# RWKV block times a routed expert layer: the experts' second product in three f32r passes instead of one f32 product

## The chip, the cores and the metric

The kernel runs on one core of a Trainium2 chip. The time is the device time of one launch in microseconds. The kernel before took 1147.42 us, the median of three runs (1146.86 to 1148.62).

## What is computed

The input is x, 16 sequences of 512 tokens with 256 channels; both branches read its layer norm xn. They are an RWKV block over the tokens of a sequence in order (time mixing with a decaying state, then channel mixing) and a layer of 8 experts in which every token goes to one expert. Cut to what matters here:

```python
x = L0_attn_x                      # (16, 512, 256): T = 8192 tokens
xn = _layernorm(x, axis=-1)
s = _L0_attn_ref(xn, ...)          # layer norms, k/v/r projections, wkv scan, Wo, channel mix
# _L0_ffn_ref(xn, Wg, W1, W2): D = 256, F = 512, E = 8
probs = jax.nn.softmax(xt @ Wg, axis=-1)
# the T // E best tokens of each expert, the rest by their largest probability: tok2exp, weights
for e in range(E):
    gate = jnp.where(tok2exp == e, weights, 0.0)
    h = jax.nn.gelu(xt @ W1[e], approximate=False) @ W2[e]
    out = out + gate[:, None] * h
g = _silu(out)
x = x + s * g
```

The change touches `... @ W2[e]`, a product over F = 512.

## The kernel before

The program has two stages. The first, some 820 us, goes through 16 blocks of 512 tokens: norms, projections, scan and channel mixing, with the router's work spread between them; its last block ends with `channel_out(NB - 1, ...)` on TensorE. It writes x and s as rows to DRAM (`xs_rows`) and a list of tokens sorted by expert, padded so that each tile of 128 tokens belongs to one expert.

The second stage, the expert stage, goes through NT = 72 such tiles. Each engine runs its own `step(t, i, g)`: six steps written out, a loop (`Fori`) of ten rounds of six, and six written out again. Engines meet only at semaphores, and each takes its instructions in the order in which they stand:

- GpSimd fetches the rows of a tile by an indirect DMA (`gather`, six tiles ahead) and stores finished rows (`scatter`).
- ScalarE in step t: `xn(t+3)` (line 690) normalises the rows with two numbers of `info_t`; `gelu(t+1)` (line 697) takes 128x512 from PSUM; `tanh(t)` (line 705) takes the second product.
- TensorE in step t: `turn_x(t+2)` (line 936) transposes; `mlp_in(t+1)` (line 946) is the first product, 8 matmuls 128x128; `mlp_out(t)` (line 957) the second, 4 matmuls 128x256 in f32.
- VectorE in step t: `mlp_input(t+3)` copies the expert's W1 (line 1507, its place read from `expert_at` into a register, line 1504) and the transposed tile out of PSUM (line 1509); `combine(t)` (lines 1519 to 1525) waits for `tanh(t)` and makes the output rows; `take_index(t+6)` (line 1436) and `take_info(t+4)` (line 1441) copy from the list.

So `xn(t+4)`, the first instruction of ScalarE's step t+1, waits (`info_ready`) for `take_info(t+4)`, the last of VectorE's step t, which stands behind `combine(t)`.

One product in the first stage is already done in three f32r passes: `hidden` splits the mixed input into a high part, rounded to f32r by ScalarE (line 589), and the rest, made by VectorE (line 1301), and multiplies high by high, high by low and low by high (lines 845 to 852). The matmul instructions of f32 stand twice in the trace for each one in the code (4 matmuls of `mlp_out` are x8), those of f32r once.

## Time and profile before

| | |
|---|---|
| median of three runs | 1147.42 us |
| the profiled execution's own time | 1145.82 us |
| its span, first to last instruction | 1144.0 us |
| TensorE busy (share of the span) | 1056.0 us (92%) |
| VectorE busy | 878.3 us (77%) |
| ScalarE busy | 627.6 us (55%) |
| GpSimd busy | 353.9 us (31%) |
| mean granted TensorE clock | 0.98 of full |

The engines' shares are means over both stages; the stage to read is the expert stage, from 850 us on. Rows of the timeline give the start, the duration and, in brackets, how long the engine had been idle and what ended that. A duration begins and ends inside the engine's pipeline, so that the next instruction of the engine can start some 0.1 us before the end shown.

### The profile page before, as it was taken

The numbers are of one execution on the slowest core, as the hardware profiler recorded it, in microseconds if no ns is written. First come the engines' busy times: TensorE is split into PE (matmuls) and PEld (weight loads), VectorE is DVE, ScalarE is ACT, GpSimd is POOL, SyncE is SP. The second block draws the span as 40 slices with busy tenths as digits, with TensorE's granted clock in tenths as the row PEclk, the third lists the DMA queues.
The fourth block names the chain that finished last, engine by engine and source line by source line (L and its number), as shares of the span: only waits on it lengthen the run. The fifth ranks groups of instructions, "written<-read, shape, count | busy, mean of one in ns | idle before, by whom it ended". The sixth has DMA issues, their size and how long they took to land.

```text
span 1144.0 us, 19481 instructions
## 1 busy us (share of the span) xinstructions
PE 1056.0 (92%) x5152; PEld 835.4 (73%) x5153; DVE 878.3 (77%) x1988; ACT 627.6 (55%) x1085; POOL 353.9 (31%) x403
## 2 busy tenths in 40 slices
PE   5689999999999999999998698989899999999997
PEld 5358777677766777767775577667788888888886
DVE  5899797988989889898898868786426666666664
ACT  2647466685765857658574557647333333433332
POOL 3122313100001000010000537364406555555563
PEclk9889999999999999999999899999999999999999
DMA  9422230110101101011010101053503333323220
GB/s 305 159 89 93 92 110 0 38 47 10 55 0 55 55 0 55 0 55 55 1 56 1 56 1 56 1 184 107 204 19 107 91 95 97 102 90 97 88 75 15
DMA packets 60054, 80.44 MB, mean 70 GB/s; under 512 B 7774, under 2 KB 47327, under 8 KB 60002
## 3 DMA queue, kind: packets, MB, share of 16 engines
q1 hardware_dynamic: 48658, 54.69, 14.7%
q0 software_dynamic: 11360, 25.32, 7.3%
q8 instruction: 17, 0.28, 0.1%
q14 instruction: 19, 0.16, 0.0%
HBM read 65.17 MB, written 26.49 MB: 80 GB/s over the span
## 4 chain that ended last, share of the span: by engine, by line
PE 55%; DVE 14%; issue 14%; ACT 11%; POOL 4%; DMA 1%; DVEq 1%; ACTq 0%; SPq 0%; POOLq 0%
PE psM L946 11%; PE psM L815 11%; PE psKV L875 11%; PE psM L957 5%; PE psR L957 5%; ACT arena L596 3%; PE psM L827 3%; DVE arena L1282 2%; POOL sorted_list L400 2%; PE psT L780 2%; ACT arena L600 2%; PE psT L936 2%; PE psR L736 2%; ACT L580 1%; ACT L574 1%
## 5 line engine op out<-in xcount | busy, mean ns | idle before, releaser
L875 PE MATMUL psKV<-arena 128*128 128x256 f32 x1024 | 236.0, 384 | 3.4 <-ACT arena L600 1.7
L875 PEld LDWEIGHTS psKV<-arena 128*128 128x128 f32 x1024 | 193.8, 192 | 42.6 <-issue 14.8
L815 PE MATMUL psM<-arena 128*128 128x512 f32 x384 | 174.2, 600 | 1.0
L407 POOL TENSOR_SCALAR lnw<-mv 128x4 f32<-128x4 f32 x32 | 8.8, 275 | 484.5 <-DVE mv L1263 484.3
L946 PE MATMUL psM<-arena 128*128 128x128 f32 x1152 | 144.3, 279 | 0.1
L946 PEld LDWEIGHTS psM<-arena 128*128 128x128 f32 x1152 | 135.8, 193 | 4.2 <-issue 1.8
L690 ACT ACTIVATE arena<-arena,info_t 128x256 f32<-128x256 f32 x72 | 43.1, 600 | 161.9 <-DVE info_t L1441 153.6
L815 PEld LDWEIGHTS psM<-arena 128*128 128x128 f32 x384 | 70.7, 192 | 81.7 <-issue 80.1
L467 POOL DMA_INDIRECT out_dram<-arena,out_idx x72 | 88.5, 1229 | 95.8 <-DVE row_idx L1436 81.9
L1282 DVE SCALAR_TENSOR_TENSOR arena<-arena,vecs 128x512 f32<-128x512 f32 x160 | 108.7, 746 | 0.0
L845 PE MATMUL psM<-mix_hi,wfk_hi 128*128 128x512 f32 x256 | 103.6, 405 | 2.5 <-ACT mix_hi L589 1.3
L510 ACT ACTIVATE arena<-s_ring,cf 128x256 f32 (+1 forms) x128 | 66.3, 591 | 68.0 <-POOL cf L412 68.0
L400 POOL DMA_INDIRECT sorted_list<-info_cur,place_cur x64 | 71.1, 1111 | 97.5 <-DVE info_cur L1239 78.6
L557 ACT ACTIVATE arena<-psM 128x512 f32<-128x512 f32 x64 | 36.5, 588 | 115.6 <-PE psM L815 115.6
L847 PE MATMUL psM<-mix_hi,wfk_lo 128*128 128x512 f32 x256 | 99.9, 390 | 0.0
L596 ACT ACTIVATE arena<-psM 128x512 f32<-128x512 f32 x128 | 74.1, 590 | 38.2 <-PE psM L852 38.0
L863 PE MATMUL psM<-arena 128*128 128x256 f32 x256 | 64.5, 396 | 24.5 <-ACT arena L596 24.5
L518 ACT ACTIVATE arena<-psT,vecs 128x512 f32<-128x512 f32 x64 | 46.4, 774 | 68.6 <-PE psT L780 68.6
L1507 DVE COPY arena<-arena 128x1024 f32 x72 | 50.4, 700 | 43.7 <-issue 41.7
L1277 DVE TENSOR_TENSOR arena<-arena 128x512 f32<-128x512 f32 x64 | 42.6, 692 | 53.3 <-ACT arena L518 53.3
L852 PE MATMUL psM<-mix_lo,wfk_hi 128*128 128x512 f32 x256 | 79.2, 390 | 0.7 <-DVE mix_lo L1301 0.7
L600 ACT ACTIVATE arena<-arena 128x512 f32<-128x512 f32 x128 | 77.1, 626 | 0.0
(191 smaller groups left out, 2006.4 us busy)
## 6 DMA issues: line engine op xcount, KB each, us to landing
desk<-in_x SPq DMA_DIRECT2D x16, 512.0 KB, 5.0
arena<-in_x SPq DMA_DIRECT2D x16, 512.0 KB, 3.8
desk<-in_xT SPq DMA_DIRECT2D x16, 512.0 KB, 4.1
xs_rows<-s_ring SPq DMA_DIRECT2D x16, 512.0 KB, 3.2
xs_rows<-in_x SPq DMA_DIRECT2D x16, 512.0 KB, 4.3
desk<-in_W SPq DMA_DIRECT2D x8, 512.0 KB, 8.3
arena<-in_W SPq DMA_DIRECT2D x8, 512.0 KB, 7.5
out_dram<-arena,out_idx POOLq DMA_INDIRECT x72, 2.8
```

Of the source, the lines that this page charges most:

```text
L400: pool.indirect_dma_start(sorted_list[:, :], bass.IndirectOffsetOnAxis(place_cur[:, j:j + 1], axis=0), info_cur[:, j, :], None).then_inc(S ...
L467: pool.indirect_dma_start(out[:, :], bass.IndirectOffsetOnAxis(out_idx[i][:, 0:1], axis=0), out_t[i], None, bounds_check=T - 1, oob_is_err ...
L596: act.activation(kf2[:, h], psM[:, h % 3, :], ACT.Relu).then_inc(S["relu_done"], 1)
L600: act.activation(kf2[:, h], kf2[:, h], ACT.Square).then_inc(S["sq_done"], 1)
L815: ins = pe.matmul(psM[:, u % 3, :], w[:, k, c * P:(c + 1) * P], mixA[:, m, k, :], start=(k == 0), stop=(k == CH - 1))
L845: pe.matmul(psM[:, h % 3, :], wfk_hi[:, k, n], mix_hi[:, k, :], start=(k == 0), stop=False)
L847: pe.matmul(psM[:, h % 3, :], wfk_lo[:, k, n], mix_hi[:, k, :], start=False, stop=False)
L852: ins = pe.matmul(psM[:, h % 3, :], wfk_hi[:, k, n], mix_lo[:, k, :], start=False, stop=(k == CH - 1))
L875: ins = pe.matmul(psKV[:, j // 2, (j % 2) * C:(j % 2 + 1) * C], kf2[:, h, j * P:(j + 1) * P], wfv[:, h, :], start=(h == 0), stop=(h == HC ...
L946: ins = pe.matmul(psM[:, i % 2, f * P:(f + 1) * P], w1_t[i % 2][:, k, f * P:(f + 1) * P], xnT[i % 2][:, k, :], start=(k == 0), stop=(k == ...
L957: ins = pe.matmul(y_ps[i % 2], hT_t[i % 2][:, f, :], w2_sb[:, ds(w + f * C, C)], start=(f == 0), stop=(f == FK - 1))
L1282: ins = v.scalar_tensor_tensor(dst[:, c], dmix[:, c], vecs[:, c, V[m]:V[m] + 1], hT[:, c, 0:SEQ], ALU.mult, ALU.add)
```

## The change

`mlp_out` becomes three f32r passes: the high part of gelu's output by the high part of W2, high by low, and low by high.

- W2 is split once, before the experts: VectorE rounds the first four experts' W2 in one copy (128x4096) and ScalarE the others' (4 copies 128x1024); VectorE makes the low parts (8 subtractions 128x1024). It starts when the last `hidden` is done (`kf_done`), since `w2_hi` lies over the channel-mix weights. TensorE waits for it (`w2_split`) before `mlp_in(0)`.
- ScalarE computes gelu twice from PSUM, once in f32 and once rounded to f32r (`hT_hi`); VectorE subtracts one from the other (`split_h`) for `hT_lo`.
- The copy of the transposed tile out of PSUM goes from VectorE to ScalarE (`take_xn`). `mlp_in` waits for `w1_taken` and `xn_taken`, `mlp_out` for `h_lo_done`.
- Buffers are laid out anew by hand; the first stage's instructions keep their order.

```diff
             def mlp_out(t, i):
...
-                wait_run(pe, S["gelu_done"], t + 1)
+                wait_run(pe, S["h_lo_done"], t + 1)
...
                 for f in range(FK):
-                    ins = pe.matmul(y_ps[i % 2], hT_t[i % 2][:, f, :], w2_sb[:, ds(w + f * C, C)],
-                                    start=(f == 0), stop=(f == FK - 1))
+                    n = slice(f * P, (f + 1) * P)
+                    pe.matmul(y_ps[i % 2], hT_hi[i % 2][:, n], w2_hi[:, ds(w + f * C, C)], start=(f == 0), stop=False)
+                    pe.matmul(y_ps[i % 2], hT_hi[i % 2][:, n], w2_lo[:, ds(w + f * C, C)], start=False, stop=False)
+                    ins = pe.matmul(y_ps[i % 2], hT_lo[i % 2][:, n], w2_hi[:, ds(w + f * C, C)],
+                                    start=False, stop=(f == FK - 1))
...
             def gelu(t, i):
...
-                act.activation(hT_t[i % 2].rearrange("p f t -> p (f t)"), psM[:, i % 2, :], ACT.Gelu
-                               ).then_inc(S["gelu_done"], 1)
+                wait_run(act, S["h_done"], t + 1)
+                act.activation(hT_t[i % 2], psM[:, i % 2, :], ACT.Gelu).then_inc(S["gelu_done"], 1)
+                act.activation(hT_hi[i % 2], psM[:, i % 2, :], ACT.Gelu).then_inc(S["h_hi_done"], 1)
...
                     gelu(t + 1, (i + 1) % RING)
+                if not isinstance(t, int) or t < NT - 2:
+                    take_xn(t + 2, (i + 2) % RING)
+                tanh(t, i)
...
+            def split_h(t, i):
+                wait_run(v, S["h_hi_done"], t + 1)
+                v.tensor_tensor(hT_lo[i % 2], hT_t[i % 2], hT_hi[i % 2].bitcast(F32), ALU.subtract
+                                ).then_inc(S["h_lo_done"], 1)
+
+            def split_w2():
+                v.wait_ge(S["w2_in"], 16 * E)
+                v.wait_ge(S["kf_done"], HC * NB)
+                whole = slice(0, W2_DVE * CH * F)
+                v.tensor_copy(w2_hi[:, whole], w2_sb[:, whole]).then_inc(S["w2_first_done"], 1)
+                for e in range(E):
+                    n = slice(e * CH * F, (e + 1) * CH * F)
+                    v.wait_ge(S["w2_first_done"], 1) if e < W2_DVE else v.wait_ge(S["w2_hi_done"], e - W2_DVE + 1)
+                    ins = v.tensor_tensor(w2_lo[:, n], w2_sb[:, n], w2_hi[:, n].bitcast(F32), ALU.subtract)
+                ins.then_inc(S["w2_split"], 1)
...
             def step(t, i, g):
+                if not isinstance(t, int) or t < NT - 1:
+                    split_h(t + 1, (i + 1) % RING)
                 if not isinstance(t, int) or t < NT - 3:
                     mlp_input(t + 3, (i + 3) % RING)
```

What VectorE issues in the loop from one `take_info` to the next `combine`, before (L1436 and L1441 are `take_index` and `take_info`, L1504 to L1509 `mlp_input`, L1519 and L1520 the start of `combine`; "waits" names semaphores):

```order
L1441 ISA
L1441 COPY info_t<-list_sb 128x4
L1504 REGISTER_ALU
L1504 TENSOR_LOAD expert_at
L1504 ISA x2
L1507 ISA [waits h_done]
L1507 COPY arena<-arena 128x1024
L1509 COPY arena<-psT 128x256 [waits turned]
L1519 ISA [waits rows_out2,tanh_done]
L1519 COPY out_idx<-list_sb 128x1
L1520 SCALAR_TENSOR_TENSOR arena<-psM,info_t,arena 128x256
```

and now (L1557 is `split_h`, L1549 and L1552 `mlp_input`, L1578 and L1579 `combine`):

```order
L1486 ISA
L1486 COPY info_t<-list_sb 128x4
L1557 TENSOR_TENSOR hT_rounded<-arena,hT_rounded 128x512 [waits h_hi_done]
L1549 REGISTER_ALU
L1549 TENSOR_LOAD expert_at
L1549 ISA x2
L1552 ISA [waits h_done]
L1552 COPY arena<-arena 128x1024
L1578 ISA [waits rows_out2,tanh_done]
L1578 COPY out_idx<-list_sb 128x1
L1579 SCALAR_TENSOR_TENSOR arena<-psM,info_t,arena 128x256
```

The subtraction stands first, with its wait for `h_hi_done`, ahead of the register load, the W1 copy and `combine`; the copy out of psT is gone.

ScalarE in the loop, one step before (L690 `xn`, L697 `gelu`, L705 `tanh`):

```order
L237 REGISTER_ALU [waits gathered5]
L690 ACTIVATE arena<-arena,info_t 128x256 [waits info_ready,turned]
L697 ACTIVATE arena<-psM 128x512 [waits y_done,h_done]
L705 ACTIVATE arena<-psM,info_t 128x256 [waits combined,y_done]
L685 ISA
L237 REGISTER_ALU [waits gathered0]
L690 ACTIVATE arena<-arena,info_t 128x256 [waits info_ready,turned]
L697 ACTIVATE arena<-psM 128x512 [waits y_done,h_done]
```

and now (L709 `xn`, L727 and L728 the two gelus, L716 `take_xn`, L735 `tanh`):

```order
L256 REGISTER_ALU [waits gathered4]
L709 ACTIVATE arena<-arena,info_t 128x256 [waits info_ready,turned]
L727 ACTIVATE arena<-psM 128x512 [waits y_done,h_done]
L728 ACTIVATE hT_rounded<-psM 128x512
L716 ACTIVATE arena<-psT 128x256 [waits turned,h_done]
L735 ACTIVATE arena<-psR,info_t 128x256 [waits combined,y_done]
L256 REGISTER_ALU [waits gathered5]
```

Two instructions stand between gelu and `tanh` that were not there.

TensorE in the last steps, the start of one `mlp_out` before:

```order
L957 ISA [waits combined,gelu_done]
L957 MATMUL psR<-desk,arena 128x256
L957 ISA
L957 MATMUL psR<-desk,arena 128x256
L957 ISA
```

and now (L1000, L1001 and L1002 are the three passes):

```order
L1000 ISA [waits combined,h_lo_done]
L1000 MATMUL psR<-w_hi,hT_rounded 128x256
L1001 REGISTER_ALU
L1001 MATMUL psR<-w_lo,hT_rounded 128x256
L1002 MATMUL psR<-w_hi,hT_rounded 128x256
L1000 ISA
L1000 MATMUL psR<-w_hi,hT_rounded 128x256
```

Each of the four matmuls has become three, with a register instruction ahead of two of them.

## Rows read from the trace of the kernel before

**Rows 1.** One window: length; busy PE, PEld, DVE, ACT, POOL; PEclk; DMA share; GB/s.

```profile
980.00:1020.00 40.00, 39.69 (x264) 35.06 (x264) 26.42 (x82) 15.63 (x31) 22.98 (x20) 1.00 0.32 97
```

**Rows 2.** Waits of the whole run: engine, line, releaser: total us, times, longest.

```profile
ACT arena L690 <- DVE info_t L1441: 153.6, 68, 4.9
```

**Rows 3.** Timeline of one expert step, all engines: start us, us, engine, line, idle before.

```profile
1003.10 0.42 DVE L1525 TENSOR_TENSOR arena<-arena 128x256 f32<-128x256 f32 x1
...
1003.93 0.60 ACT L690 ACTIVATE arena<-arena,info_t 128x256 f32<-128x256 f32 x1 [2.35 <-DVE info_t L1441]
...
1004.43 0.73 DVE L1507 COPY arena<-arena 128x1024 f32 x1 [0.77 <-issue]
...
1004.43 0.58 ACT L697 ACTIVATE arena<-psM 128x512 f32<-128x512 f32 x1
...
1004.82 0.41 PE L936 MATMUL psT<-cst,arena 128*128 128x128 f32 x2
...
1004.91 0.46 ACT L705 ACTIVATE arena<-psR,info_t 128x256 f32<-128x256 f32 x1
...
1005.16 2.02 PE L946 MATMUL psM<-arena 128*128 128x128 f32 x16
...
1005.69 0.47 DVE L1520 SCALAR_TENSOR_TENSOR arena<-psR,info_t,arena 128x256 f32<-128x256 f32 x1
...
1006.32 0.43 DVE L1523 SCALAR_TENSOR_TENSOR arena<-arena 128x256 f32<-128x256 f32 x1 [0.15 <-DVE arena L1520]
...
1007.02 1.89 PE L957 MATMUL psM<-desk,arena 128*128 x8
...
1007.66 0.60 ACT L690 ACTIVATE arena<-arena,info_t 128x256 f32<-128x256 f32 x1 [2.28 <-DVE info_t L1441]
...
1008.75 0.38 PE L936 MATMUL psT<-cst,arena 128*128 128x128 f32 x2
```

**Rows 4.** VectorE groups by line, 870 to 1120 us: busy us, mean ns, idle before.

```profile
L1507 DVE COPY arena<-arena 128x1024 f32 x64 | 44.7, 699 | 40.9 <-issue 40.9
```

**Rows 5.** Line 1504 on VectorE's sequencer, 1003.2 to 1005 us: ns, first and last start.

```profile
L1504 DVEq TENSOR_LOAD <-expert_at x1: 315/315/315, 1003.5 to 1003.5; - x1
```

**Rows 6.** Lines 589 and 1301, the split of the mixed input: ns min/median/max, starts.

```profile
L589 ACT ACTIVATE mix_hi<-arena x32: 615/630/632, 83.4 to 818.0; 128x512 fp32r<-128x512 f32 x32
...
L1301 DVE TENSOR_TENSOR mix_lo<-arena,mix_hi x32: 677/684/712, 85.3 to 819.8; 128x512 fp32r<-128x512 f32 x32
```

**Rows 7.** Timeline of TensorE in the three f32r passes of line 845.

```profile
783.39 0.39 PE L845 MATMUL psM<-mix_hi,wfk_hi 128*128 128x512 f32 x1
...
783.62 0.39 PE L847 MATMUL psM<-mix_hi,wfk_lo 128*128 128x512 f32 x1
```

**Rows 8.** Timeline of TensorE between the last hidden layer and the first expert tile.

```profile
830.20 0.62 PE L852 MATMUL psM<-mix_lo,wfk_hi 128*128 128x512 f32 x2
...
850.36 1.95 PE L946 MATMUL psM<-arena 128*128 128x128 f32 x16
```

**Rows 9.** Line 1415, a 128x1024 sum on VectorE: ns min/median/max, starts.

```profile
L1415 DVE TENSOR_TENSOR s_ring<-s_ring,arena x16: 1224/1226/1230, 149.5 to 851.8; 128x1024 f32<-128x1024 f32 x9, 128x1024 f32 x7
```

**Rows 10.** Timeline of ScalarE and TensorE at the start of the steady steps.

```profile
861.44 0.60 ACT L690 ACTIVATE arena<-arena,info_t 128x256 f32<-128x256 f32 x1 [4.88 <-DVE info_t L1441]
...
862.09 0.44 PE L936 MATMUL psT<-cst,arena 128*128 128x128 f32 x2 [2.32 <-ACT arena L690]
...
862.36 3.52 PE L946 MATMUL psM<-arena 128*128 128x128 f32 x16
```

**Rows 11.** Timeline of VectorE and ScalarE in the last steps, behind the loop.

```profile
1123.56 0.47 DVE L1520 SCALAR_TENSOR_TENSOR arena<-psR,info_t,arena 128x256 f32<-128x256 f32 x1
...
1124.53 0.42 DVE L1525 TENSOR_TENSOR arena<-arena 128x256 f32<-128x256 f32 x1
...
1125.12 0.60 ACT L690 ACTIVATE arena<-arena,info_t 128x256 f32<-128x256 f32 x1 [1.73 <-DVE info_t L1441]
...
1125.27 0.69 DVE L1507 COPY arena<-arena 128x1024 f32 x1 [0.24 <-issue]
```

More of the change, by code:

```diff
@@ L89, in rwkv_times_moe, with planned, same_place @@
     with ExitStack() as ctx:
+        home = {}
+        def planned(name, shape, dt=F32):
+            words = math.prod(shape[1:])
+            home[name] = nc.bump_sbuf(4 * words)[0]
+            return nc.alloc_sbuf_tensor_at(name, shape, dt, offset=home[name])
+        def same_place(name, words, other, first=0):
+            return nc.alloc_sbuf_tensor_at(name, [P, words], F32R, offset=home[other] + 4 * first)
+        ARENA = 28169
+        DESK = 10240
+        arena = planned("arena", [P, ARENA])
+        desk = planned("desk", [P, DESK])
+        wk, wv, wr, wo = (planned(n, [P, CH, C]) for n in ("wk", "wv", "wr", "wo"))
+        mix_hi, mix_lo = (planned(n, [P, CH, SEQ], F32R) for n in ("mix_hi", "mix_lo"))
+        wfk_hi, wfk_lo = (planned(n, [P, CH, HID], F32R) for n in ("wfk_hi", "wfk_lo"))
+        assert home["wfk_lo"] + 4 * CH * HID == home["wk"] + 4 * E * CH * F
         def sb(name, shape, dt=F32):
@@ L199, in rwkv_times_moe @@
         w1_t = [a.rearrange("p (k f) -> p k f", k=CH) for a in ring(CH * F, 2)]
-        hT_t = [a.rearrange("p (f t) -> p f t", f=FK) for a in ring(F, 2)]
+        hT_rounded = same_place("hT_rounded", 4 * F, "arena", rc[0])
+        hT_hi = [hT_rounded[:, i * F:(i + 1) * F] for i in (0, 1)]
+        hT_lo = [hT_rounded[:, i * F:(i + 1) * F] for i in (3, 2)]
+        ring(F, 2)
+        hT_t = ring(F, 2)
         th_t = ring(C, 2)
@@ L691, in xn, with take_xn, split_w2 @@
                                ).then_inc(S["xn_done"], 1)
+            def take_xn(t, i):
+                wait_run(act, S["turned"], t + 1)
+                if not (isinstance(t, int) and t < 2):
+                    wait_run(act, S["h_done"], t - 1)
+                act.activation(xnT[i % 2].rearrange("p k t -> p (k t)"), psT[:, i % 2, 0:C], ACT.Copy
+                               ).then_inc(S["xn_taken"], 1)
+            def split_w2(e):
+                n = slice(e * CH * F, (e + 1) * CH * F)
+                act.activation(w2_hi[:, n], w2_sb[:, n], ACT.Copy).then_inc(S["w2_hi_done"], 1)
             def gelu(t, i):
@@ L708, in step @@
             def step(t, i, g):
-                if not isinstance(t, int) or -3 <= t < NT - 3:
+                if not isinstance(t, int) or t < NT - 3:
                     xn(t + 3, (i + 3) % RING, g + (i + 3) // RING)
-                if not isinstance(t, int) or -1 <= t < NT - 1:
+                if not isinstance(t, int) or t < NT - 1:
                     gelu(t + 1, (i + 1) % RING)
-                if not isinstance(t, int) or t >= 0:
-                    tanh(t, i)
-            steps(act, step)
+                if not isinstance(t, int) or t < NT - 2:
+                    take_xn(t + 2, (i + 2) % RING)
+                tanh(t, i)
+            xn(0, 0, 0)
+            xn(1, 1, 0)
+            act.wait_ge(S["w2_in"], 16 * E)
+            act.wait_ge(S["kf_done"], HC * NB)
+            for e in range(W2_DVE, E):
+                split_w2(e)
+            take_xn(0, 0)
+            take_xn(1, 1)
+            xn(2, 2, 0)
+            gelu(0, 0)
+            steps(act, step, 0)
         @block.tensor
@@ L1542, in _ @@
             mlp_input(1, 1)
+            split_w2()
             gate_out(NB - 1)
             residual2(NB - 1)
+            take_info(3, 3)
+            split_h(0, 0)
             mlp_input(2, 2)
-            take_info(3, 3)
             steps(v, step, 0)
```

42 lines of the change are left out of this document (20 added, 22 removed).

## The prediction

> **What bounds the kernel now.** I first read which stage the change touches: the expert stage, 72 tiles from 850 us on. The busy table of one 40 us window there shows TensorE at 39.69 of 40 us at full granted clock, VectorE at 26.42 and ScalarE at 15.63 [rows 1]. Read alone, that says that only TensorE matters. The list of waits says more: ScalarE stood 153.6 us, 68 times, before `xn` (line 690), released by VectorE's `take_info` (line 1441) [rows 2]. Such a wait costs nothing while ScalarE has slack, but it may be part of a ring that closes once per tile. So the third view is the timeline of one step, where both paths can be added up [rows 3].
>
> TensorE's path: two transposes from 1004.82 to 1005.16 (0.34), first product to 1007.02 (1.86), second product to 1008.75 (1.73). Sum 3.93 us.
>
> The ring: `xn(t+4)` starts at 1003.93, gelu 0.50 later (1004.43), `tanh` 0.48 after that (1004.91), VectorE's first multiply of `combine` 0.78 later (1005.69), and 1.97 after it, with the rest of `combine`, the two list copies and the release, the next `xn` (1007.66). Sum 3.73 us. It closes because `xn` stands ahead of gelu on ScalarE and `take_info` behind `combine` on VectorE.
>
> From `xn(4)` at 861.44 [rows 10] to `xn(71)` at 1125.12 [rows 11] there are 67 steps in 263.7 us, 3.94 each: TensorE's sum. The ring lies only 0.2 us below it, so it has hardly any room for what is added.
>
> **The change, part by part.**
>
> *The second product.* Removed: 8 trace instructions 128x256 of f32 (1.73 us). Added: 12 of f32r. No row shows an f32r pass of 256 columns. Passes of 512 columns follow one another at 0.23 us (783.39 to 783.62) [rows 7], so half the columns would be 0.115; the nearest row with a weight load for each short matmul is the first product, 1.86 / 16 = 0.116 [rows 3]. I take 0.116: 12 x 0.116 = 1.39, a gain of 0.34 us on TensorE. The upper end is 0.23 each, 2.76 us, a loss of 1.03. TensorE's step becomes 0.34 + 1.86 + 1.39 = 3.59 us (4.96 at the upper end). The added register instructions go into the same bounds.
>
> *The second gelu.* It stands before `take_xn` and `tanh`. ScalarE's spacing of such an instruction is 0.48, its duration 0.58 [rows 3]; a rounding copy 128x512 took 0.63 [rows 6]. I take 0.58 to its end, at most 0.63.
>
> *`take_xn`.* It adds 0.46 at most (as `tanh`, same shape, from PSUM [rows 3]) ahead of `tanh`. VectorE will reach `combine` later than that (below), so it lies beside VectorE's work. Does TensorE wait for it? Counted from `xn`, it starts at 0.50 + 0.48 + 0.48 = 1.46 and ends at 1.92; `mlp_in(t+2)` then runs from about 2.0 to 3.9, and its result is wanted by the next gelu, one step plus 0.50 after `xn`. With the step below that is 1.9 us of cover.
>
> *`split_h`, the new wait.* VectorE now stands before the subtraction until `h_hi_done`, and behind it in line are the register load, the W1 copy, `combine` and `take_info`, for which ScalarE's next `xn` waits. Before, the load and the W1 copy lay in the time in which gelu and `tanh` ran. Now all of it comes after the second gelu. The ring is then:
>
> - `xn` to gelu 0.50, gelu to second gelu 0.48, its duration 0.58 [rows 3];
> - release of VectorE 0.15, the idle time of a VectorE instruction in the loop that waits for a semaphore (line 1523) [rows 3]; behind the loop such a release costs about 0.05. Bounds 0.05 and 0.15;
> - from the start of the subtraction to the start of the W1 copy. The subtraction itself is 0.68 (line 1301, same shape and types) [rows 6], 0.60 before the next can start. But the W1 copy needs the expert's place from a register load. In the step shown the load starts at 1003.5 [rows 5], not before line 1525 has started (1003.10), although nothing that it reads is late, and the copy starts at 1004.43 [rows 3], 0.93 later. The engine idled 0.77 there, against 40.9 / 64 = 0.64 in the mean [rows 4], so 0.80 is the usual distance. The load would start some 0.10 after the subtraction. I take 0.90; bounds 0.60 (load hidden) and 1.0;
> - W1 copy 0.70 [rows 4], up to the first multiply of `combine` (the 0.15 us copy between them overlaps both). `tanh` has long ended then (2.4 against about 3.3 after `xn`);
> - from that multiply to the next `xn` 1.97, as before.
>
> Sum 0.50 + 0.48 + 0.58 + 0.15 + 0.90 + 0.70 + 1.97 = 5.28 us; low end 4.88, high end 5.43. That is more than TensorE's 3.59, and more than its upper end 4.96, so the price of the f32r pass drops out of the forecast. The copy out of psT (0.43) that leaves VectorE gives nothing back: it lay in the `tanh` wait.
>
> Here a rule speaks for the low end. The Trainium skill, "Perfetto Trace Analysis", section "DVE / Act Engine Instruction", has the sequencer push a waiting instruction into a wait queue and go on with the next. By it the load would run under the wait and the ring be 4.98. The row of the load, behind a waiting instruction, speaks against that in the loop.
>
> *Steps outside the loop.* Of the 67 distances from `xn(4)` to `xn(71)`, 60 lie in the loop; 5 before and 2 behind it are written out. There the multiply comes 1.56 before the next `xn` (1123.56 to 1125.12), and the W1 copy 0.74 after line 1525's start (1124.53 to 1125.27) [rows 11]. Ring: 0.50 + 0.48 + 0.58 + 0.05 + 0.74 + 0.70 + 1.56 = 4.61 us.
>
> *W2's split.* It can start when the last `hidden` ends, at 830.82, and TensorE needs it at 850.36 [rows 8]. VectorE's 8 subtractions 128x1024 are 8 x 1.23 = 9.8 us [rows 9]. Its rounding copy of 4096 columns is 4 x 0.70 = 2.8 us by the W1 copy [rows 4], at most 4 x 1.23 = 4.9. Ready between 843.4 and 845.5: cover 4.9 us and more, under TensorE's last `channel_out`, price nothing. ScalarE's four roundings, at 2 x 0.63 each [rows 6], are 5 us, before VectorE asks for the last. Were the cover gone, each microsecond late would come on top. Moving buffers changes no instruction of the first stage: nothing.
>
> *Sum.* `combine(0)` waits for a gather that nothing here moves, so `xn(4)` stays at 861.44 [rows 10]. `xn(71)`: 861.44 + 60 x 5.28 + 7 x 4.61 = 1210.5. Before, 18.9 us followed (1125.12 to 1144.0); the last tile's second gelu and subtraction add about 1.3: 20.2. Span 1230.7, against 1144.0. The profiled execution took 1.8 more than its span, and the median of the runs lies 1.6 above it: 1234 us, 7.5% slower.
>
> **The rivals.**
>
> *The ring does not close as I read it* (the other side, faster): ScalarE's `xn` finds its `info_t` early, the 153.6 us being mere slack. Then the longest path is TensorE's or the one over `take_xn`: `take_xn` 0.46, release 0.1, first product 1.95, release 0.1, two gelus 0.96 = 3.57 us. 67 x (3.94 - 3.57) = 25 us less: 1122. The mean of 3.94 equal to TensorE's sum speaks for it; that `xn` starts 0.2 to 0.3 after `take_info` in each step, and the queue orders shown, speak against it. It decides where the ring is under 3.94, and it is 1.3 above.
>
> *An f32r pass is no cheaper than the weight load and its registers let it be*, the change not doing what it says. At 0.23 each TensorE needs 4.96: without the ring 67 x 1.02 = 68 us more, 1216; with the ring no difference. Neither row settles it; it matters only together with the first rival.
>
> *The clock falls.* TensorE would be idle 1.7 of 5.28 us. After a stop of 2.32 us the first product took 3.52 us instead of 2.02 [rows 3, 10], the lower of the two levels of the clock, 1.2 GHz. All at that level: 0.44 + 3.5 + 12 x 0.23 = 6.7 us per step, and the bound moves to TensorE: 60 x 1.4 = 84 more, 1318; in half of the steps 1276. Against it: the longest single stop I expect is about 1.1 us (before the first product, waiting for `take_xn`), and a TensorE that is the bound is busy throughout, which brought the clock back above. The Trainium skill, "TensorE: Matmul & The Clock Gate", section "Loop structure matters more than you think", warns that frequent small stops between groups of matmuls can make the clock swing; no row here shows it for stops of 1 us.
>
> **How the numbers follow.** The ring at 4.88 to 5.43: 0.83, with its own range of 1208 to 1244. Clock in at least a good part of the steps: 0.07. The ring not closed: 0.05 at 1122, and 0.02 for the same with dear passes or a gain eaten up elsewhere. 0.03 for mishaps that end above 1244, a late split of W2 or a dearer first stage. The range 1204 to 1256 holds the first case and the near part of the clock's. Faster by over 0.2% (what a measurement of this kernel can tell from no change): 0.05; within it 0.02; slower 0.93.
>
> **What would show it.** The distance from one `xn` (now line 709) to the next in the loop, 5.28 us. ScalarE's wait before it for `info_t` grows from 2.3 to about 3 us. VectorE's W1 copy starts 0.9 after the subtraction, with idle time put down to "issue". TensorE's busy share in the windows falls to some seven tenths at a granted clock of 1.00, with its waits before the first product released by ScalarE; its 12 passes take about 1.4 us. The first expert product starts at 850 us as before. I am wrong if the distance is at 3.6 or 3.9, if the granted clock in the expert stage is well below 1, or if TensorE has no gap.

## The result and the profile after

| | before | after |
|---|---|---|
| median | 1147.68 us | 1236.96 us (1236.41 to 1237.81, 4 runs) |
| ratio | | 1.078 (95%: 1.0764 to 1.0796) |
| span of the profiled execution | 1144.0 us | 1234.6 us |
| TensorE busy | 1056.0 us (92%) | 1052.4 us (85%) |
| VectorE busy | 878.3 us (77%) | 905.4 us (73%) |
| ScalarE busy | 627.6 us (55%) | 681.1 us (55%) |
| mean granted TensorE clock | 0.98 | 0.98 |

The kernel before was timed again beside it, on the same chip. The change makes the kernel 89 us slower. TensorE does no more work than before, VectorE 27 and ScalarE 54 us more, and no engine is full; the time went into waiting. One window of the expert stage, columns as in [rows 1]:

```profile
980.00:1020.00 40.00, 29.73 (x237) 27.01 (x235) 21.95 (x63) 15.46 (x35) 19.24 (x15) 1.00 0.24 73
```

TensorE is busy 29.73 of 40 us instead of 39.69, at full granted clock. The list of waits from 870 to 1200 us says for what each engine stood (total us, times, longest):

```profile
ACT arena L709 <- DVE info_t L1486: 184.5, 60, 3.5
...
DVE hT_rounded L1557 <- ACT hT_rounded L728: 118.8, 62, 2.0
...
PE psM L988 <- ACT arena L716: 48.7, 60, 0.8
PE psT L977 <- ACT arena L709: 38.5, 58, 1.0
```

Each of these four comes about 60 times, once per step of the loop. ScalarE waits 3.1 us per step for `take_info`, 2.3 before [rows 2]. VectorE, which had no such wait in that place, stands 1.9 us per step before the subtraction, released by the second gelu. TensorE waits twice, 0.8 and 0.6, both times for ScalarE. All engines waiting for one another, none of them full, is what a ring looks like in this view. One step of it, all engines, against [rows 3]:

```profile
1004.01 0.60 ACT L709 ACTIVATE arena<-arena,info_t 128x256 f32<-128x256 f32 x1 [3.07 <-DVE info_t L1486]
...
1004.52 0.58 ACT L727 ACTIVATE arena<-psM 128x512 f32<-128x512 f32 x1
...
1004.91 0.41 PE L977 MATMUL psT<-cst,arena 128*128 128x128 f32 x2 [0.60 <-ACT arena L709]
1005.00 0.59 ACT L728 ACTIVATE hT_rounded<-psM 128x512 fp32r<-128x512 f32 x1
1005.48 0.38 ACT L716 ACTIVATE arena<-psT 128x256 f32<-128x256 f32 x1
1005.73 0.69 DVE L1557 TENSOR_TENSOR hT_rounded<-arena,hT_rounded 128x512 fp32r<-128x512 f32 x1 [1.92 <-ACT hT_rounded L728]
...
1006.15 2.02 PE L988 MATMUL psM<-arena 128*128 128x128 f32 x16 [0.83 <-ACT arena L716]
1006.65 0.70 DVE L1552 COPY arena<-arena 128x1024 f32 x1 [0.22 <-issue]
...
1007.32 0.47 DVE L1579 SCALAR_TENSOR_TENSOR arena<-psM,info_t,arena 128x256 f32<-128x256 f32 x1
...
1007.93 0.36 PE L1000 MATMUL psR<-w_hi,hT_rounded 128*128 x1
...
1008.92 0.16 DVE L1486 COPY info_t<-list_sb 128x4 f32 x1
...
1009.29 0.60 ACT L709 ACTIVATE arena<-arena,info_t 128x256 f32<-128x256 f32 x1 [3.06 <-DVE info_t L1486]
1009.31 0.28 PE L1002 MATMUL psR<-w_hi,hT_rounded 128*128 x1
```

Read it along the ring: `xn` 1004.01, gelu +0.51, second gelu +0.48, subtraction +0.73 (the gelu's 0.59 and a release of 0.14), W1 copy +0.92, first multiply of `combine` +0.67, next `xn` +1.97. That is 5.28 us, and no instruction on this way waits for anything else. The 12 passes of the second product start from 1007.93 to 1009.31, about 0.12 us apart, and lie beside VectorE's `combine`.

The register load for the W1 copy, answering to [rows 5]: it starts at 1005.8, when the subtraction before it has started (1005.73), not during VectorE's 1.92 us of waiting.

```profile
L1549 DVEq TENSOR_LOAD <-expert_at x1: 301/301/301, 1005.8 to 1005.8; - x1
```

W2's split, between the last hidden layer and the first expert tile, answering to [rows 8, 9]:

```profile
831.07 0.62 PE L893 MATMUL psM<-mix_lo,wfk_hi 128*128 128x512 f32 x2
...
831.80 2.29 DVE L1564 CAST w_hi<-desk 128x4096 fp32r<-128x4096 f32 x1 [6.12 <-PE psM L893]
...
834.13 9.28 DVE L1568 TENSOR_TENSOR w_lo<-desk,w_hi 128x1024 fp32r<-128x1024 f32 x8
...
851.23 1.95 PE L988 MATMUL psM<-arena 128*128 128x128 f32 x16
...
862.21 0.60 ACT L709 ACTIVATE arena<-arena,info_t 128x256 f32<-128x256 f32 x1 [4.87 <-DVE info_t L1486]
...
864.16 3.76 PE L988 MATMUL psM<-arena 128*128 128x128 f32 x16 [0.85 <-issue]
```

The split is over at 843.4; TensorE asks for it at 851.23, 0.9 us later than before because the whole first stage runs 0.8 to 0.9 us later (its last `hidden` at 831.07 instead of 830.20). The last two rows answer to [rows 10]: `xn(4)` is 0.77 later, and the first product after the pause of the start runs at the lower of the clock's two levels again (3.76 us for 16 matmuls, granted clock 0.50 from 864 to 868 us).

The end, answering to [rows 11], `xn(71)`:

```profile
1214.70 0.60 ACT L709 ACTIVATE arena<-arena,info_t 128x256 f32<-128x256 f32 x1 [2.38 <-issue]
```

From 862.21 to 1214.70 there are 67 steps in 352.5 us. The distances repeat every six steps in the loop: 5.28, 5.28, 5.28, 5.34, 5.38, 5.29 (mean 5.31). Before, they were 263.7 us. So 88.8 of the 90.6 us by which the span grew lie in these 67 distances, 0.8 ahead of them and 1.0 behind.

### The profile page after: what moved, and what is told of

Read it like the earlier page. It is cut to its first block and busy times, and to the rows that moved or that the text cites. A ratio compares the mean times of both kernels' runs of the same rounds, so it can differ in the third digit from the quotient of the medians.

```text
span 1234.6 us, 20795 instructions
## 1 busy us (share of the span) xinstructions
PE 1052.4 (85%) x5440; PEld 836.5 (68%) x5441; DVE 905.4 (73%) x1997; ACT 681.1 (55%) x1233; POOL 371.2 (30%) x403
## 5 line engine op out<-in xcount | busy, mean ns | idle before, releaser
L988 PE MATMUL psM<-arena 128*128 128x128 f32 x1152 | 147.1, 281 | 54.6 <-ACT arena L716 48.7
L988 PEld LDWEIGHTS psM<-arena 128*128 128x128 f32 x1152 | 135.7, 193 | 68.8 <-issue 68.8
L709 ACT ACTIVATE arena<-arena,info_t 128x256 f32<-128x256 f32 x72 | 43.1, 600 | 207.5 <-DVE info_t L1486 192.5
L1557 DVE TENSOR_TENSOR hT_rounded<-arena,hT_rounded 128x512 fp32r<-128x512 f32 x72 | 49.9, 693 | 132.8 <-ACT hT_rounded L728 132.8
L486 POOL DMA_INDIRECT out_dram<-arena,out_idx x72 | 73.2, 1016 | 168.0 <-DVE row_idx L1481 152.1
L473 POOL DMA_INDIRECT arena<-xs_rows,row_idx x66 | 100.3, 1519 | 23.1 <-issue 23.1
L904 PEld LDWEIGHTS psM<-arena 128*128 128x128 f32 x256 | 47.7, 194 | 36.6 <-ACT arena L615 30.7
```

Of the source, the lines that this page charges most:

```text
L473: pool.indirect_dma_start(rows[i][:, columns], None, source, bass.IndirectOffsetOnAxis(row_idx[i][:, 0:1], axis=0), bounds_check=T - 1, oo ...
L486: pool.indirect_dma_start(out[:, :], bass.IndirectOffsetOnAxis(out_idx[i][:, 0:1], axis=0), out_t[i], None, bounds_check=T - 1, oob_is_err ...
L904: ins = pe.matmul(psM[:, (HC + u) % 3, (j % 2) * C:(j % 2 + 1) * C], mixB_r[:, k, j * P:(j + 1) * P], wfr[:, k, :], start=(k == 0), stop=( ...
L988: ins = pe.matmul(psM[:, i % 2, f * P:(f + 1) * P], w1_t[i % 2][:, k, f * P:(f + 1) * P], xnT[i % 2][:, k, :], start=(k == 0), stop=(k == ...
```

## The experiments

The theory: the step is the ring `xn` → gelu → second gelu → subtraction → W1 copy → `combine` → `take_info` → `xn`, and everything else is off the path. The rivals: it is the price of the passes; it is ScalarE's or VectorE's added work as such; it is the clock. The ring has several places at which it can be cut, stretched or shortened; each was tried. Kernels named "after" start from the changed kernel, "before" from the one before it. The ratio is always against the kernel before, run on the same chip between them.

**Cut the ring at `take_info` (after).**

```diff
             def step(t, i, g):
+                if not isinstance(t, int) or t < NT - 4:
+                    take_info(t + 4, (i + 4) % RING)
                 if not isinstance(t, int) or t < NT - 1:
                     split_h(t + 1, (i + 1) % RING)
...
-                if not isinstance(t, int) or t < NT - 4:
-                    take_info(t + 4, (i + 4) % RING)
```

> The changed kernel with VectorE's take_info(t+4) moved from the end of its step to the start, ahead of split_h; nothing else. Theory (the ring xn, two gelus, subtraction, register load, W1 copy, combine, take_info, xn sets 5.28 us a step): the ring is cut, and what is left is the loop over take_xn and the first product, 3.7 us, and TensorE's 3.6. Step 3.7, so 67 x (5.26 - 3.70) = 105 us less than 1237: about 1132, faster than the kernel before. Rival (VectorE and ScalarE simply have more work per tile, or TensorE's passes are dear, and the order does not matter): within a few us of 1237.

Measured: 1142.9 us, ratio 0.9958 (0.9941 to 0.9974). Moving one 128x4 copy from the end of VectorE's step to its start takes 94 us away, all that the change had cost and 5 more, with passes, second gelu, subtraction and `take_xn` all still there. The price of the work as such is refuted. The size was missed by 11 us: 1132 stood on a loop over `take_xn` estimated at 3.7 us. Its rows:

```profile
1004.55 2.02 PE L988 MATMUL psM<-arena 128*128 128x128 f32 x16
...
1006.70 0.60 ACT L727 ACTIVATE arena<-psM 128x512 f32<-128x512 f32 x1 [0.29 <-PE psM L988]
...
1007.19 0.59 ACT L728 ACTIVATE hT_rounded<-psM 128x512 fp32r<-128x512 f32 x1
...
1007.67 0.39 ACT L716 ACTIVATE arena<-psT 128x256 f32<-128x256 f32 x1
...
1008.35 0.35 PE L988 MATMUL psM<-arena 128*128 128x128 f32 x1 [0.19 <-issue]
```

First product to gelu 2.15, two spacings of a gelu 0.49 and 0.48, `take_xn` 0.39, release and turn 0.29: 3.80 us. This second ring, first product → gelus → `take_xn` → first product, is what was next in line, and the two releases in it are 0.2 to 0.3, not 0.1.

**The same edit on the kernel before.**

```diff
             def step(t, i, g):
+                if not isinstance(t, int) or t < NT - 4:
+                    take_info(t + 4, (i + 4) % RING)
                 if not isinstance(t, int) or t < NT - 3:
                     mlp_input(t + 3, (i + 3) % RING)
...
-                if not isinstance(t, int) or t < NT - 4:
-                    take_info(t + 4, (i + 4) % RING)
```

> The kernel before with take_info(t+4) moved to the start of VectorE's step in the same way. Theory: its ring of 3.73 us lay under TensorE's 3.93, so nothing is to be had: 1144 to 1148. Rival (ScalarE's wait for info_t of 153.6 us was itself time on the path): well below that, towards 1120.

Measured: 1137.88 us, ratio 0.9914 (0.9898 to 0.9931). Missed: it gains 10 us. TensorE's step in it:

```profile
1005.00 0.38 PE L936 MATMUL psT<-cst,arena 128*128 128x128 f32 x2
...
1005.21 1.95 PE L946 MATMUL psM<-arena 128*128 128x128 f32 x16
...
1007.00 1.89 PE L957 MATMUL psR<-desk,arena 128*128 x8
...
1008.73 0.38 PE L936 MATMUL psT<-cst,arena 128*128 128x128 f32 x2
```

0.21 + 1.79 + 1.73 = 3.73 us, with the window full:

```profile
1000.00:1040.00 40.00, 40.00 (x280) 37.24 (x279) 28.37 (x87) 17.51 (x32) 24.19 (x21) 1.00 0.33 99
```

TensorE's own sum was therefore 3.73, not the 3.93 of [rows 3]: transposes and first product took 0.13 and 0.07 longer there (0.41 and 2.02 us instead of 0.38 and 1.95). The matmul row shows no idle time before them, but the row of weight loads does: before the transposes at 1004.82 it had stood 0.48 us, because `xn` had ended only at 1004.53. Over a window the busy row hid that (39.69 against 40.00) and the weight loads did not (35.06 against 37.24).

A one-step ring of 3.73 and an engine of 3.73 do not add up to steps of 3.94 (from `xn` to `xn` they go between 3.73 and 4.26, mean 3.95 from 941 to 1059 us). A path that I had not summed does: it runs through both engines and closes after two steps. The rows of the kernel before that complete those of [rows 3], with the weight loads just named:

```profile
1004.79 0.20 PEld L936 LDWEIGHTS psT<-cst,arena 128*128 128x128 f32 x2 [0.48 <-issue]
...
1009.04 0.47 ACT L705 ACTIVATE arena<-psM,info_t 128x256 f32<-128x256 f32 x1 [0.30 <-PE psM L957]
...
1011.79 0.60 ACT L690 ACTIVATE arena<-arena,info_t 128x256 f32<-128x256 f32 x1 [2.28 <-DVE info_t L1441]
```

From `xn` (1003.93) 0.89 to the transposes that waited for it, 0.34 to the first product, 1.86 to the second, 2.02 to the `tanh` that waited for it (1009.04), 0.78 to `combine`, 1.97 over `take_info` to the `xn` two steps on (1011.79): 7.86 us for two steps, 3.93 each. This ring too goes over `take_info`, so the same edit cut it as well, and the 10 us gained fit. The sum is read from the rows; no run cuts this ring alone.

With `take_info` moved in both kernels the changed one is 5 us behind the other (1142.9, 1137.9): so much is left of the 89 us once the rings over `take_info` are gone.

**The price of the passes: the second product as 4 f32 matmuls (after).**

```diff
-                    pe.matmul(y_ps[i % 2], hT_hi[i % 2][:, n], w2_hi[:, ds(w + f * C, C)], start=(f == 0), stop=False)
-                    pe.matmul(y_ps[i % 2], hT_hi[i % 2][:, n], w2_lo[:, ds(w + f * C, C)], start=False, stop=False)
-                    ins = pe.matmul(y_ps[i % 2], hT_lo[i % 2][:, n], w2_hi[:, ds(w + f * C, C)],
-                                    start=False, stop=(f == FK - 1))
+                    ins = pe.matmul(y_ps[i % 2], hT_hi[i % 2][:, n].bitcast(F32),
+                                    w2_hi[:, ds(w + f * C, C)].bitcast(F32), start=(f == 0), stop=(f == FK - 1))
```

> The changed kernel with the second product as 4 f32 matmuls of the high parts alone (the low parts are still made and waited for, but left out of the product). Theory: TensorE's step goes from 3.59 back to 3.93, all under the ring's 5.28: no change from 1237 within 2 us. Rival (the passes' price, their register instructions or their reads are part of the loss): moves by 67 x the difference per tile, 5 us or more.

Measured: 1238.43 us, ratio 1.0791 (1.0773 to 1.0809), the same as after. The product takes 1.89 us again and the step stays at 5.28:

```profile
1000.00 0.41 PE L977 MATMUL psT<-cst,arena 128*128 128x128 f32 x2 [0.29 <-ACT arena L709]
...
1003.10 1.89 PE L1000 MATMUL psM<-w_hi,hT_rounded 128*128 x8
...
1005.28 0.30 PE L977 MATMUL psT<-cst,arena 128*128 128x128 f32 x1 [0.29 <-ACT arena L709]
```

What a pass costs is settled by the rows (0.12 us) and does not matter here.

**`take_xn` alone (before).**

```diff
-                v.tensor_copy(xnT[i % 2].rearrange("p k t -> p (k t)"), psT[:, i % 2, 0:C]
-                              ).then_inc(S["mlp_in_ready"], 1)
...
+            def take_xn(t, i):
...
+                act.activation(xnT[i % 2].rearrange("p k t -> p (k t)"), psT[:, i % 2, 0:C], ACT.Copy
+                               ).then_inc(S["xn_taken"], 1)
...
                     gelu(t + 1, (i + 1) % RING)
+                if not isinstance(t, int) or t < NT - 2:
+                    take_xn(t + 2, (i + 2) % RING)
```

> The kernel before with one part of the change alone: the copy of the transposed tile goes from VectorE to ScalarE, behind gelu. Theory: the ring of 3.73 gets 0.26 us longer (the spacing from this copy to tanh in the changed kernel), 3.99 in the loop against TensorE's 3.93: 3 to 5 us slower, 1151. Rival (VectorE relieved of 0.43 us per tile is a gain; or ScalarE's new place in TensorE's path costs): under 1145, or over 1160.

Measured: 1159.7 us, ratio 1.0104 (1.0087 to 1.012). Right in sign, three times the size, and at the very edge of the rival's "over 1160", so the time alone does not tell the two apart. The rows do. The steps alternate between 3.9 and 4.3 (mean 4.13 from 941 to 1057 us), and the path over two steps now goes through `take_xn`:

```profile
1011.57 0.60 ACT L690 ACTIVATE arena<-arena,info_t 128x256 f32<-128x256 f32 x1 [2.29 <-DVE info_t L1456]
...
1013.22 2.02 PE L961 MATMUL psM<-arena 128*128 128x128 f32 x16
...
1017.09 0.47 ACT L712 ACTIVATE arena<-psM,info_t 128x256 f32<-128x256 f32 x1
...
1019.85 0.60 ACT L690 ACTIVATE arena<-arena,info_t 128x256 f32<-128x256 f32 x1 [2.29 <-DVE info_t L1456]
```

From `xn` 0.50 to gelu, 0.48 to `take_xn`, 0.67 to the first product that waited for it, 1.86 to the second product, 2.01 to `tanh`, 0.79 to `combine`, 1.97 to `xn`: 8.28 us for two steps, 4.14 each. The expectation had lengthened only the one-step ring, to 3.99. The rival's half on ScalarE's new place in TensorE's path was the right one. (The edit also writes out ScalarE's first instructions in a new order and splits one semaphore in two, as the change does; 12.3 of the 13.8 us by which the span grew lie in the 67 distances between `xn(4)` and `xn(71)`.)

**The subtraction at the end of VectorE's step (after).**

```diff
             def step(t, i, g):
-                if not isinstance(t, int) or t < NT - 1:
-                    split_h(t + 1, (i + 1) % RING)
...
                     take_info(t + 4, (i + 4) % RING)
+                if not isinstance(t, int) or t < NT - 1:
+                    split_h(t + 1, (i + 1) % RING)
```

> The changed kernel with split_h(t+1) moved from the start of VectorE's step to its end, behind take_info; nothing else. Theory: the subtraction, the load behind it and the W1 copy leave the ring, which becomes the old 3.73 plus the second gelu's spacing 0.48 and take_xn's 0.26, 4.47 us. The second product now waits for a subtraction that starts only then, so TensorE may add some tenths (e7 added 0.1 where two paths were close). Step 4.47 to 4.8: 1237 - 67 x (5.26 - 4.6) = 1193, within 1184 to 1206. Rival (what counts is the work of VectorE and ScalarE, the same here): 1237.

Measured: 1246.72 us, ratio 1.0873 (1.0855 to 1.0891). Missed by 54 us, on the wrong side of after. The rows show a ring that I had not counted:

```profile
1006.06 0.69 DVE L1557 TENSOR_TENSOR hT_rounded<-arena,hT_rounded 128x512 fp32r<-128x512 f32 x1
...
1007.18 0.38 PE L1000 MATMUL psM<-w_hi,hT_rounded 128*128 x1 [1.68 <-DVE hT_rounded L1557]
...
1009.60 0.15 DVE L1578 COPY out_idx<-list_sb 128x1 int32 x1 [2.08 <-ACT arena L735]
...
1011.35 0.68 DVE L1557 TENSOR_TENSOR hT_rounded<-arena,hT_rounded 128x512 fp32r<-128x512 f32 x1
```

The subtraction for tile t+1 now stands behind `combine(t)`; TensorE's second product waits for it (1.68), `tanh(t+1)` for the product, `combine(t+1)` for `tanh` (VectorE idle 2.08), and behind it stands the next subtraction: 5.29 in the step shown, 5.38 in the mean of the loop. The ring through `take_info` was gone, and one as long through `mlp_out` had taken its place. My sum had followed only the engine from which I took the work.

**The register load ahead of the subtraction (after).**

```diff
             def step(t, i, g):
+                w = w1_place(t + 3) if not isinstance(t, int) or t < NT - 3 else None
                 if not isinstance(t, int) or t < NT - 1:
                     split_h(t + 1, (i + 1) % RING)
                 if not isinstance(t, int) or t < NT - 3:
-                    mlp_input(t + 3, (i + 3) % RING)
+                    mlp_input(t + 3, (i + 3) % RING, w)
```

> The changed kernel with the register load of the expert's place issued ahead of the wait of split_h, at the start of VectorE's step; nothing else. Theory: in the loop the W1 copy starts 0.92 us after the subtraction, 0.23 of it idle, since the load stands behind a waiting instruction; with the load first it follows at 0.62 to 0.7. 60 x 0.23 to 0.3 = 14 to 18 us less than 1237: about 1221. Rival (the sequencer runs past the wait anyway, and the idle 0.23 has another cause): 1237.

Measured: 1216.74 us, ratio 1.0606 (1.0588 to 1.0623): 20 us less than after. The W1 copy follows the subtraction at 0.61 instead of 0.92:

```profile
1003.71 0.69 DVE L1561 TENSOR_TENSOR hT_rounded<-arena,hT_rounded 128x512 fp32r<-128x512 f32 x1 [1.93 <-ACT hT_rounded L728]
...
1004.32 0.69 DVE L1556 COPY arena<-arena 128x1024 f32 x1
```

60 x 0.31 = 18.6 us, so a term of the ring's sum moves the time one for one. The gain is 4 us more than forecast.

**`take_xn` ahead of gelu (after).**

```diff
-                if not isinstance(t, int) or t < NT - 1:
-                    gelu(t + 1, (i + 1) % RING)
                 if not isinstance(t, int) or t < NT - 2:
                     take_xn(t + 2, (i + 2) % RING)
+                if not isinstance(t, int) or t < NT - 1:
+                    gelu(t + 1, (i + 1) % RING)
```

> The changed kernel with take_xn(t+2) ahead of gelu(t+1) on ScalarE instead of behind both gelus; the same instructions. Theory: the copy, which lay beside VectorE's work, comes into the ring between xn and the first gelu, at its spacing of 0.26 to 0.33: 67 x 0.3 = 20 us more than 1237, about 1256. Rival (TensorE, which waits for this copy before each first product, sets the time): it gets the tile 1 us earlier, so faster than 1237.

Measured: 1260.41 us, ratio 1.0987 (1.0969 to 1.1005), 23 us more than after, in the forecast direction and 4 us beyond it. The step is 5.70 instead of 5.28. Of these 0.42 us 0.26 are the copy's spacing between `xn` and gelu (0.77 instead of 0.51), as expected; 0.16 came between the subtraction and the W1 copy (1.08 instead of 0.92), which I did not expect and no run explains. This kernel also had the clock in it:

```profile
1000.00:1040.00 40.00, 30.15 (x212) 27.45 (x211) 19.77 (x57) 15.44 (x35) 14.23 (x15) 0.91 0.22 67
```

```profile
1004.32 0.41 PE L977 MATMUL psT<-cst,arena 128*128 128x128 f32 x2 [1.79 <-ACT arena L716]
...
1004.77 3.04 PE L988 MATMUL psM<-arena 128*128 128x128 f32 x16
```

Granted clock 0.91 in the window; the first product took 3.04 us instead of 2.02 after TensorE had stood 1.79 us. It lies beside the ring: TensorE still stood idle a quarter of the window, and the next step, whose first product took 2.02 us again, was no shorter (5.73).

**`xn` behind the gelus (after), the ring cut at its other end.**

```diff
-                if not isinstance(t, int) or t < NT - 3:
-                    xn(t + 3, (i + 3) % RING, g + (i + 3) // RING)
...
                     take_xn(t + 2, (i + 2) % RING)
+                if not isinstance(t, int) or t < NT - 3:
+                    xn(t + 3, (i + 3) % RING, g + (i + 3) // RING)
                 tanh(t, i)
```

> The changed kernel with ScalarE's xn(t+3) moved from the start of its step to behind both gelus and take_xn, ahead of tanh; VectorE's order as in the changed kernel. Theory: the ring is cut at its other end, as gelu no longer stands behind the xn that waits for take_info. But TensorE's transposes wait for xn, and the first product stands behind them: gelu to xn's end 0.48 + 0.48 + 0.27 + 0.60, release and transposes 0.6, first product to the next gelu 2.15, 4.6 us in all. 1237 - 67 x (5.26 - 4.6) = 1193, within 1185 to 1200. Rival (the wait for info_t as such costs, wherever xn stands): 1237.

Measured: 1201.32 us, ratio 1.0473 (1.0456 to 1.0491), 1 us above the range given. Gelu comes every 4.73 us (1003.89 to 1008.62), the way now being gelus, `take_xn`, `xn`, transposes (TensorE waited 0.90 for `xn`), first product.

**Both cuts that the rings ask for: `take_info` first and `take_xn` ahead of gelu (after).** On top of the first experiment:

```diff
-                if not isinstance(t, int) or t < NT - 1:
-                    gelu(t + 1, (i + 1) % RING)
                 if not isinstance(t, int) or t < NT - 2:
                     take_xn(t + 2, (i + 2) % RING)
+                if not isinstance(t, int) or t < NT - 1:
+                    gelu(t + 1, (i + 1) % RING)
```

> e1 (take_info first on VectorE) with the same exchange as in e10, take_xn(t+2) ahead of gelu(t+1). Here the ring is cut, and the loop take_xn, first product, two gelus, take_xn of 3.80 us set e1's step. Theory: the loop loses both gelus, and the longest is then VectorE's own round (subtraction to W1 copy 0.92, to combine 0.67, to the end of the list copies 1.77, release 0.15) at 3.5, before TensorE's 3.4 (0.22 + 1.79 + 12 x 0.116): 1143 - 67 x 0.3 = 1123. Rival (an exchange of two ScalarE instructions adds to e1 what it adds in e10): slower than 1143. Should GpSimd's gathers set the step, for which xn waited 68 us in e1, it stays at 1135 to 1143.

Measured: 1141.69 us, ratio 0.9956 (0.9939 to 0.9972). Not 1123: the clause on the gathers held. `xn` now waits for the rows themselves (the gather was issued at 1007.47):

```profile
1011.15 0.60 ACT L709 ACTIVATE arena<-arena,info_t 128x256 f32<-128x256 f32 x1 [2.32 <-DMA arena<-xs_rows,row_idx]
```

```profile
ACT arena L709 <- DMA arena<-xs_rows,row_idx: 93.1, 63, 5.6
```

**The same with the register load first.** On top of the last:

```diff
+                w = w1_place(t + 3) if not isinstance(t, int) or t < NT - 3 else None
                 if not isinstance(t, int) or t < NT - 1:
                     split_h(t + 1, (i + 1) % RING)
...
-                    mlp_input(t + 3, (i + 3) % RING)
+                    mlp_input(t + 3, (i + 3) % RING, w)
```

> e8 with the register load ahead of split_h as in e5. In e8 the step was 3.76 on average, but its xn waited 84 us for gathers: a ring over three steps, from combine(t) over the scatter and the gather of tile t+6 on GpSimd to xn(t+6). Theory of that ring: the shorter load lies in it (gelu, subtraction, load, W1 copy, combine), 0.23 to 0.3 in three steps, so 0.1 per step, 7 us: about 1135. Rival (VectorE's round of 3.5 was the bound): 0.23 per step, 15 us less than e8's 1142: about 1126.

Measured: 1137.19 us, ratio 0.9915 (0.9899 to 0.9932). VectorE's path got 0.3 us shorter and only 4.5 us came of it: VectorE was not the bound.

**The gather ahead of the scatter on GpSimd, on the kernel of the last experiment.**

```diff
                 for i in range(RING):
-                    scatter(RING * g + i, i)
+                    wait_run(pool, S["combined"], RING * g + i + 1)
                     gather(RING * g + (RING + i), i)
+                    scatter(RING * g + i, i)
```

> e9 with GpSimd's gather of tile t+6 issued ahead of the scatter of tile t (both wait for combine(t)). Theory: the scatter's 1.0 to 1.5 us and the 0.3 between them leave the three-step ring, 0.45 per step, and the step falls to TensorE's or VectorE's 3.4 to 3.5: 1112 to 1122. Rival (the gathers only come late because the steps are, and do not hold them): no change from e9.

Measured: 1126.57 us, ratio 0.9823 (0.9807 to 0.984), 10.6 us less than the kernel it starts from, though 5 us above the range given. The way of a row buffer (`combine`, scatter, gather, landing, `xn`) was the third ring. What stands last now is VectorE itself: its subtraction starts every 3.5 us in four of six steps (3.66 in the mean), with idle time of 0.4 to 0.5 put down to "issue", behind the register load, which here stands directly ahead of it:

```profile
1006.32 0.69 DVE L1562 TENSOR_TENSOR hT_rounded<-arena,hT_rounded 128x512 fp32r<-128x512 f32 x1 [0.45 <-issue]
...
1009.85 0.69 DVE L1562 TENSOR_TENSOR hT_rounded<-arena,hT_rounded 128x512 fp32r<-128x512 f32 x1 [0.46 <-issue]
```

**So the load goes back behind the subtraction.** 

```diff
-                w = w1_place(t + 3) if not isinstance(t, int) or t < NT - 3 else None
...
-                    mlp_input(t + 3, (i + 3) % RING, w)
+                    mlp_input(t + 3, (i + 3) % RING)
```

> e13 without the early register load, so e8 (take_info first, take_xn ahead of gelu) with the gather ahead of the scatter. In e13 a step took 3.5 us, VectorE's round, with 0.45 us idle ahead of each subtraction, put to issue: there the early load is exposed. Theory: with the load behind the subtraction the round is 0.07 + 0.93 + 0.67 + 1.65 = 3.3, and TensorE's 3.4 becomes the bound: 60 x 0.1 = 6 us less than e13's 1127, about 1120. Rival (what e5 gained holds here too): 60 x 0.3 more, 1140 or above.

Measured: 1118.84 us (1117.59 to 1120.31, 5 runs), ratio 0.9752 (0.9739 to 0.9765). The same load, 20 us dear behind the subtraction while the long ring stood, is worth 8 us there now. The subtraction no longer stands waiting for long (6.4 us in 14 waits from 880 to 1100 us, against 1.9 us per step in the changed kernel), so a load ahead of it has no wait to run under and shows in full (30.8 us idle in 58 steps); behind it, it runs partly under the subtraction (12.6 us in 46).

```profile
1000.00:1040.00 40.00, 39.68 (x344) 39.13 (x343) 32.34 (x92) 26.96 (x58) 26.82 (x23) 1.00 0.36 109
```

TensorE is busy throughout, and its weight loads 39.13 of 40 us. The step is 3.5 us in the mean (344 matmuls, 30 to a step, in 40 us), against 3.94 before. By the sums of the rows the passes take TensorE's own step from 3.73 to 3.4 us (0.22 + 1.79 + 12 x 0.116), and three waits had to be out of the way before that could show. Not all of the 2.5% is theirs: moving `take_info` alone gave the kernel before 0.9914, and what the gather's new place would give it was not run. Of all kernels run this is the fastest, 9.5% under the changed one (0.9752 / 1.078).

## Why the prediction was right, and where not

Forecast 1234, range 1204 to 1256; measured 1236.96.

- *The ring as the bound*: shown. Its terms 0.50, 0.48, 0.58, 0.15, 0.90, 0.70, 1.97 measured 0.51, 0.48, 0.59, 0.14, 0.92, 0.67, 1.97. Cut at `take_info` it gave 94 us back, shortened by 0.31 it gave 20, stretched by 0.42 it took 23, and with TensorE's part of the work changed it did not move.
- *5.28 in the loop*: 5.28 in four of six steps, 5.31 in the mean; 60 x 0.03 = 1.8 us of the 3 us by which I was low. In the fourth step the excess is in the last term (2.03 instead of 1.97), in the fifth between subtraction and W1 copy (1.02 instead of 0.92); the second is gone in the kernel with the register load first (4.97), the first is not (5.03). What causes them stays open.
- *Outside the loop* 4.61: the last two distances, whose steps are written out, are 4.57 and 4.59; of the first seven, four are 4.63 to 4.82 and three 5.48 to 5.78, during the start.
- *`xn(4)` unmoved at 861.44*: off by 0.77. The lag is there from the start (the first output of the k, v and r projections is taken at 34.2 instead of 33.5 us) and the first stage adds little to it. In the traces of the other variants of the changed kernel, which share that first stage, `xn(0)` starts between 835.96 and 838.77 us (836.72 in the changed kernel), so 0.77 is within what traces of one first stage differ by.
- *The tail* 20.2: 19.9.
- *W2's split hidden*: ready at 843.4, the early end of the range; needed at 851.23.
- *The register load*: I chose the trace's row over the rule. The Trainium skill, "Perfetto Trace Analysis", section "DVE / Act Engine Instruction", has the sequencer free once the waiting instruction is in the wait queue; the ring would then be 4.98 and the time some 18 us less. The load at 1005.8, behind the waiting subtraction's start, and the 20 us of the experiment on it decide for the row: the load did not start under the wait.
- *The f32r pass at 0.116*: 0.12 in the rows; and as said, its price fell out (the f32 product in its place gave the same time).
- *The clock*: no fall in the loop of after (1.00 from 900 to 1200 us), as forecast. The chance given to it was not idle: with `take_xn` ahead of gelu the window's clock was 0.91. The Trainium skill, "TensorE: Matmul & The Clock Gate", section "A second HAM failure mode: psum-queue depth-cycling", describes a kernel in which frequent short idle times between groups of matmuls made the clock go back and forth; the section that the prediction names, "Loop structure matters more than you think", has only a long DMA wait as its example. The experiment agrees with the first: 2.02 us became 3.04 in one step and was 2.02 again in the next. It shows beside it that this costs nothing while TensorE has slack.

What failed is the first paragraph: *"67 steps in 263.7 us, 3.94 each: TensorE's sum"*. It was not TensorE's sum. That is 3.73, as the cut in the kernel before showed; 3.93 was a third path, the ring over two steps, whose sum happens to equal TensorE's sum with its hidden waits in it. 10 us of that kernel's time were already a ring's. It did the forecast no harm, because after the change the long ring stood alone; that is luck as far as this step goes. But it made me expect no gain from cutting the ring before (1144 to 1148; 1138), and too small a loss from `take_xn` alone (1151; 1160). I had read a busy share of 39.69 as full. The Trainium skill, "Perfetto Trace Analysis", section "Identifying the Most-Contended Engine", calls matmul busy time no good measure of how close TensorE is to its limit and asks for the weight loads' share. Here the trace agrees, between kernels with the same matmuls: 35.06 of 40 us before and 37.24 with the ring cut; with three passes 27.01 in the changed kernel and 39.13 in the fastest.

The first rival's price of 1122 was low for another reason: the loop over `take_xn`, there estimated at 3.57, measured 3.80, from two releases of 0.2 to 0.3 us between ScalarE and TensorE that I had put at 0.1. With the long ring cut, the changed kernel took 1143.

Open: what the gather ahead of the scatter would give the kernel before, since it was only tried on the changed one; and a run that cuts the ring over two steps and leaves the one-step ring alone.

## What to carry to other kernels

When an instruction with a new wait is put into an engine's row, follow what is queued behind it until the way comes back to the instruction itself: the sum round that ring is the step's floor, whatever the busy shares say. A ring may take more than one step to close: follow it through every engine and divide by the steps. In this kernel work added inside the ring counted in full and a change beside it not at all (the second product in f32: 1238 against 1237), and a move of one tiny copy can be worth more than the arithmetic that was changed. After a cut, sum the next ring, and the one after it, before expecting the gain: behind the ring of 5.28 here stood one of 3.80, and one through the gathers of about as much.

## What the hardware showed that was not expected

- VectorE's sequencer did not start a register load behind an instruction that waited for a semaphore; it started 0.07 us after that instruction did (1005.73, 1005.8). It was the same in the steps written out behind the loop (1207.14, 1207.2, after a wait of 1.69). With the load put ahead of it, the next copy followed 0.31 us sooner.
- The length of a stop alone did not tell the clock. With the subtraction last, TensorE stopped for up to 1.78 us in steps of 5.29 to 5.48 and the granted clock from 920 to 1210 us was 1.00; after the one stop of 1.91 us, which ended at 893.55, it was 0.70 (895 to 900 us, first product 2.94). With `take_xn` ahead of gelu, in steps of 5.70, a stop of 1.62 us was followed by a first product of 3.65 us.
- A rounding copy of 128x4096 from f32 to f32r took 2.29 us on VectorE, 0.57 per 1024 columns, where the 128x1024 copy of W1 alone took 0.70.
- A matmul row whose input came a moment late can read longer (2.02 instead of 1.95, 0.41 instead of 0.38) without idle time shown before it; the weight load's row of the same group showed the wait (0.48 us at 1004.79 in the kernel before).
